# Another order of the engines' calls in the first block and the first two heads, and no filler transpositions outside the first loads

## The reference

```python
# layer 1: one causal attention head of width 256, with its own norm
x_norm = norm(x) * gamma + beta
q, k, v = x_norm @ qkv[:, :256], x_norm @ qkv[:, 256:512], x_norm @ qkv[:, 512:]
attn = softmax(causal(q @ k.T / 16))
x = norm(x + (attn @ v @ o_proj + x))
# layer 2: 16 causal heads of width 128 with rotary embedding, then 4 experts, top 2 of them
h = x + attention(norm(x) * ln1_w + ln1_b)      # q, k, v with biases; wo, bo
m = experts(norm(h) * ln2_w + ln2_b)            # gate, gelu(h @ we1 + be1) @ we2 + be2
x = norm(x + (h + m))
```

## Time and profile before

| | |
|---|---|
| runs | 1158.55, 1160.10, 1160.26 us |
| the profiled execution: first to last instruction | 1159.9 us |
| busy: PE, weight loads of PE (PEld), DVE | 1127.7, 1024.2, 860.5 us |
| busy: ACT, POOL | 735.7, 637.3 us |
| mean granted clock of PE | 0.991 |

### The profile page before, as it was taken

How to read it: one execution, slowest core, us unless ns; L and a number is a source line. 1 busy time by engine, 2 the same in 40 slices (tenths; PEclk the granted TensorE clock), 3 DMA queues, 4 the chain that set the end, 5 groups by cost and what they waited for, 6 DMA issues and landing times.

```text
span 1159.9 us, 20549 instructions
## 1 busy us (share of the span) xinstructions
PE 1127.7 (97%) x7183; PEld 1024.2 (88%) x7183; DVE 860.5 (74%) x2016; ACT 735.7 (63%) x1565; POOL 637.3 (55%) x511
## 2 busy tenths in 40 slices
PE   7998899999999999999999999999999999989996
PEld 6997889999999999899999999999999998778995
DVE  5865767777777777777777777777777777877698
ACT  3556676666666666666666666666666665665753
POOL 2306455565656565656555555665655555846673
PEclk8999999999999999999999999999999999989998
DMA  5002221221122111212121212121212111221001
GB/s 169 1 1 82 60 54 43 52 60 37 38 54 64 40 43 46 60 37 52 43 63 37 51 37 60 37 51 37 60 37 51 37 42 46 65 91 37 1 19 55
DMA packets 46301, 56.55 MB, mean 49 GB/s; under 512 B 5940, under 2 KB 29176, under 8 KB 46200
## 3 DMA queue, kind: packets, MB, share of 16 engines
q1 hardware_dynamic: 45368, 54.19, 18.9%
q10 hardware_dynamic: 832, 1.05, 0.3%
HBM read 17.47 MB, written 4.19 MB: 19 GB/s over the span
## 4 chain that ended last, share of the span: by engine, by line
PE 84%; DVE 7%; POOL 3%; issue 3%; ACT 1%; DMA 1%; SPq 0%; ACTq 0%; POOLq 0%; DVEq 0%
PE ps_m L424 52%; PE ps_s L424 20%; PE ps_t L566 11%; DVE acc L1664 2%; DVE acc L1674 1%; POOL work L2077 1%; DVE acc L1603 1%; POOL work L2081 1%; DVE stats L1442 1%; POOL qk_lo L2088 1%; PE ps_m L477 0%; DMA work<-in_L_attn_qkv 0%; DVE rows L1495 0%; POOL hT_lo L2059 0%; PE ps_m L628 0%
## 5 line engine op out<-in xcount | busy, mean ns | idle before, releaser
L2077 POOL TENSOR_TENSOR work<-work,rope 128x512 f32<-128x512 f32 x128 | 166.7, 1303 | 232.8 <-DMA work<-work 232.8
L1570 DVE TENSOR_TENSOR pT_lo<-ps_t,pT_hi 128x512 fp32r<-128x512 f32 (+3 forms) x408 | 210.4, 550 | 36.6 <-ACT pT_hi L1073 34.3
L1073 ACT ACTIVATE pT_hi<-ps_t 128x512 fp32r<-128x512 f32 (+3 forms) x408 | 183.0, 489 | 77.7 <-PE ps_t L566 77.5
L1563 DVE CUSTOM_DVE_ANT_0 ps_s<-ps_s,causal 128x128 f32<-128x128 f32 (+7 forms) x272 | 203.1, 766 | 5.7 <-PE ps_s L424 3.2
L2081 POOL TENSOR_TENSOR work<-work 128x512 f32<-128x512 f32 x128 | 167.4, 1308 | 10.1
L2088 POOL TENSOR_TENSOR qk_lo<-work,qk_hi 128x512 fp32r<-128x512 f32 x128 | 162.7, 1292 | 18.5 <-ACT qk_hi L1030 18.5
L1603 DVE SCALAR_TENSOR_TENSOR acc<-ps_m,rinv,acc 128x256 f32<-128x256 f32 x272 | 118.5, 477 | 71.8 <-PE ps_m L424 71.7
L1024 ACT ACTIVATE work<-ps_m,bqk 128x512 f32<-128x512 f32 x128 | 88.7, 693 | 108.7 <-PE ps_m L424 108.6
L1066 ACT ACTIVATE prob_b<-ps_s,nmax 128x640 f32<-128x640 f32 (+3 forms) x136 | 130.4, 959 | 22.3 <-DVE nmax L1563 19.0
L424 PE MATMUL ps_s<-qk_hi 128*128 128x384 f32 (+5 forms) x384 | 141.0, 367 | 2.0 <-POOL qk_lo L2088 1.1
L1524 DVE SCALAR_TENSOR_TENSOR work<-ps_m,bqk,rope 128x512 f32<-128x512 f32 x128 | 95.5, 746 | 56.3 <-ACT work L1024 56.1
(11 more groups left out here) (201 smaller groups left out, 2856.5 us busy)
## 6 DMA issues: line engine op xcount, KB each, us to landing
work<-work SPq DMA_DIRECT2D x256, 128.0 KB, 2.3
acc<-in_L_attn_x SPq DMA_DIRECT2D x8, 256.0 KB, 4.7
wst<-in_L_ffn_wq SPq DMA_DIRECT2D x16, 128.0 KB, 2.5
wst<-in_L_ffn_wk SPq DMA_DIRECT2D x16, 128.0 KB, 2.4
wo_st<-in_L_ffn_wo SPq DMA_DIRECT2D x16, 128.0 KB, 2.1
wst<-in_L_ffn_wv SPq DMA_DIRECT2D x8, 256.0 KB, 3.0
x_rows<-acc SPq DMA_DIRECT2D x4, 512.0 KB, 3.4
wst<-in_L_ffn_we SPq DMA_DIRECT2D x8, 256.0 KB, 2.8
```

The costliest lines, as they stand in the source:

```text
L1073: act.activation(pT_hi[:, slots, cols], t_bank(u, i, j)[:, 0:size * P].rearrange("p (j q) -> p j q", q=P), ACT.Copy).then_inc(t_hi.sem, t_ ...
L1563: dve.tensor_tensor_reduce(s, s, causal[:, T - (i + 1) * P:T], -1.0, ABOVE_ALL, ALU.add, ALU.min, accum_out=nmax[:, u % 2, i:i + 1]).then_ ...
L1570: dve.tensor_tensor(pT_lo[:, slots, cols], t_bank(u, i, j)[:, 0:size * P].rearrange("p (j q) -> p j q", q=P), pT_hi[:, slots, cols].bitcas ...
L2077: pool.tensor_tensor(qs[:, x % 2, :], qs[:, x % 2, :], sin_t[:, c * CH:(c + 1) * CH], ALU.mult).then_inc(sin_done.sem, sin_done.up(u, x))
```

## The change

All instructions but the filler ones stay, with the same operands. Their order in the `start()` list of each engine and of the SP queue is another. Of the fillers, the 14 and 28 of `fold_weight(0)` and `vectors(0)`, during the first loads, stay; 7 at `project_q(2, 2)`, 5 at `scores(33, 0)`, 13 at `outputs(33, 1)` and 4 at `gate_logits(0, 0)` go.

```diff
@@ PE, the fillers
                     if u == 2 and x % 2 == 0:
-                        if x == 2:
-                            keep_busy(out, 7)
                         await_hT(2, c)
...
-                if (u, i) == (LAST, 0):
-                    keep_busy(all_scores[:, score_bank(u, i)[0][0]:], 5)
...
-                if (u, c) == (LAST, 1):
-                    keep_busy(out, 13)
...
-                if (b, c) == (0, 0):
-                    keep_busy(out, 4)
@@ PE, start()
                 vectors(0)
                 fold_weight(2)
                 ln_transpose(0, 0)
-                vectors(1)
                 fold_product(3)
                 fold_product(4)
+                vectors(1)
                 project_q(0, 0)
                 project_q(0, 1)
                 ln_transpose(0, 1)
+                project_v(0, 0)
                 scores(0, 0)
+                project_v(0, 1)
                 scores(0, 1)
-                project_v(0, 0)
-                project_v(0, 1)
+                project_q(0, 2)
+                project_q(0, 3)
                 scores(0, 2)
...
                 ln_transpose(2, 0)
                 scores(1, 6)
+                first_outputs(1, 0, 1)
                 project_v(1, 3)
                 project_q(2, 0)
+                transposes(1, 4)
+                ln_transpose(2, 1)
                 scores(1, 7)
-                ln_transpose(2, 1)
+                project_q(2, 1)
                 transposes(1, 5)
-                project_q(2, 1)
                 project_q(2, 2)
                 project_v(2, 0)
                 transposes(1, 6)
                 first_outputs(1, 1, 0)
+                project_q(2, 3)
+                transposes(1, 7)
                 scores(2, 0)
+                project_v(2, 1)
                 scores(2, 1)
-                project_q(2, 3)
+                project_v(2, 2)
+                transposes(2, 0)
                 scores(2, 2)
...
@@ ACT, start()
                 high_proj()
-                high_qk_weights(0, 0)
                 ln_affine(0, 0)
...
+                ln_rows(2, 1)
                 exponent(1, 5)
+                high_v_weights(0)
                 high_values(1, 3)
                 add_bias(2, 0)
-                high_v_weights(0)
-                ln_rows(2, 1)
+                high_p(1, 4)
                 ln_affine(2, 1)
+                exponent(1, 6)
+                add_bias(2, 1)
                 high_p(1, 5)
-                add_bias(2, 1)
-                exponent(1, 6)
+                add_bias(2, 2)
+                high_qk(2, 0)
+                double(1, 1)
+                high_p(1, 6)
+                high_values(2, 0)
                 exponent(1, 7)
-                high_qk(2, 0)
-                add_bias(2, 2)
...
@@ DVE, start()
                 ln_stats(0, 0)
-                ln_stats(0, 1)
                 low_fold(0)
                 low_fold(1)
                 ln_apply(0, 0)
                 copy_vectors(0)
+                ln_stats(0, 1)
                 low_fold(2)
-                copy_vectors(1)
                 split_first(0)
                 low_fold(3)
                 low_fold(4)
+                copy_vectors(1)
                 ln_apply(0, 1)
...
@@ POOL, start()
                 ln_power(2, 0)
+                low_o_weights(0, 0)
                 ln_power(2, 1)
                 ln_low(2, 0)
+                ln_low(2, 1)
                 low_v_weights(0)
-                ln_low(2, 1)
+                turn(2, 0)
+                low_qk(2, 0)
+                turn(2, 1)
+                low_qk(2, 1)
                 ln_power(3, 0)
-                turn(2, 0)
-                turn(2, 1)
-                low_qk(2, 0)
-                low_qk(2, 1)
-                low_o_weights(0, 0)
...
@@ SP, start()
                 load_rope()
+                swap(2, 0)
+                keep_x1(0, 0)
                 load_v_weights(1)
                 load_qk_weights(0, 1)
-                swap(2, 0)
+                load_o_weights(0, 1)
                 swap(2, 1)
-                keep_x1(0, 1)
-                keep_x1(0, 0)
                 swap(2, 2)
...
```

More of the change, by code:

```diff
@@ L717, in start @@
                 scores(1, 4)
+                project_v(1, 2)
+                first_outputs(1, 0, 0)
                 transposes(1, 2)
@@ L736, in start @@
                 first_outputs(1, 1, 0)
+                project_q(2, 3)
+                transposes(1, 7)
                 scores(2, 0)
+                project_v(2, 1)
                 scores(2, 1)
-                project_q(2, 3)
+                project_v(2, 2)
+                transposes(2, 0)
                 scores(2, 2)
-                project_v(2, 1)
+                first_outputs(1, 1, 1)
                 scores(2, 3)
[L743 to L748, removed]
+                project_q(3, 0)
                 transposes(2, 1)
-                project_q(3, 0)
-                scores(2, 6)
                 project_v(2, 3)
                 transposes(2, 2)
+                scores(2, 4)
+                project_q(3, 1)
                 transposes(2, 3)
-                project_q(3, 1)
+                scores(2, 5)
+                scores(2, 6)
                 outputs(2, 0)
@@ L758, in start @@
                 ln_transpose(3, 0)
+                transposes(2, 5)
+                project_q(3, 2)
                 out_project(2, 0, 0)
-                project_q(3, 2)
+                scores(2, 7)
                 out_project(2, 0, 1)
[L762 to L765, removed]
                 project_q(3, 3)
                 project_v(3, 0)
+                scores(3, 0)
                 transposes(2, 6)
+                scores(3, 1)
                 ln_transpose(3, 1)
@@ L1182, in start @@
+                exponent(1, 1)
+                high_first(1, 3)
+                high_p(1, 0)
+                exponent(1, 2)
+                high_o_weights(0, 0)
+                exponent(1, 3)
+                high_values(1, 0)
+                high_p(1, 1)
+                high_values(1, 1)
+                high_values(1, 2)
+                ln_rows(2, 0)
                 exponent(1, 4)
-                double(1, 0)
                 high_p(1, 2)
                 high_p(1, 3)
-                high_values(1, 2)
@@ L1199, in start @@
-                exponent(1, 6)
-                exponent(1, 7)
-                high_qk(2, 0)
-                add_bias(2, 2)
-                high_values(2, 0)
+                add_bias(2, 2)
[3 more added lines that the diff above has]
+                high_values(2, 0)
+                exponent(1, 7)
+                high_qk(2, 1)
+                add_bias(2, 3)
+                high_p(1, 7)
+                exponent(2, 0)
+                high_values(2, 1)
@@ L1204, in start @@
+                high_values(2, 2)
                 high_qk_weights(0, 1)
-                high_qk(2, 1)
-                high_p(1, 6)
                 high_qk(2, 2)
-                add_bias(2, 3)
-                high_values(2, 1)
-                exponent(2, 0)
+                ln_rows(3, 0)
+                high_p(2, 0)
                 exponent(2, 1)
-                high_values(2, 2)
-                high_p(1, 7)
+                high_qk(2, 3)
                 exponent(2, 2)
+                add_bias(3, 0)
@@ L1788, in start @@
+                low_p(2, 4)
                 row_max(2, 6)
-                low_o(2, 0)
+                ln_apply(3, 1)
+                rotate(3, 2)
                 accumulate(2, 0, 0)
-                low_p(2, 4)
-                rotate(3, 2)
                 accumulate(2, 0, 1)
-                add_value_bias(0, 1)
                 row_max(2, 7)
-                row_max(3, 0)
                 low_p(2, 5)
                 rotate(3, 3)
-                invert(2, 1)
                 low_values(3, 0)
+                low_p(2, 6)
```

217 lines of the change are left out of this document (100 added, 117 removed).

## The result

The changed kernel takes 1149.55 us (median of six runs, 1149.16 to 1155.01), the kernel before 1159.42 us (six runs, 1158.33 to 1160.26). The ratio is 0.9927 with a 95% interval from 0.9914 to 0.9940. The gain is 9.9 us by the medians and 8.3 us by the means (1159.35 to 1151.03); the forecast was 6.3. Its 1153.6 us is 4 us too high, inside its range.

The account below looks back on a forecast made before the run. PE, busy 97% of the span, was taken as the bound, with 13.8 us idle in `start()` to win. 2.4 + 4.8 - 0.9 = 6.3 us off 1159.9 gave 1153.6 us, range 1148.3 to 1159.

Parts of the forecast that it names:

- I count from 1159.9 and correct nothing: Whole kernel: profiled span 1159.9 us, 0.2 below the median run of 1160.1, taken as the base without correction.
- The first 20 us: Start of `start()`: first projection at about 17.5 in place of 20.90, 3.4 us earlier; worth 2.4 after 1.0 for clock.
- The term for the clock: First stretch: a low-clock stretch as likely as not in the new order, so 1.0 of 2.0 us is given back.
- 20 to 165 us: Rest of `start()`: 8.2 us of PE idle time less 3.4 of new waits, a gain of 4.8 us.
- the single waits: PE between 20 and 165 us: new waits found call by call in the reordered lists, sum 3.4 us.
- the pair at `project_v(2, 0)`: `project_v(2, 0)` and `transposes(1, 6)` wait for `rotate(2, 1)` and `low_p(1, 5)` behind DVE's `ln_stats(3, 0)`: 0.6 us.
- no new waits: Rival for `start()`: the new waits are hidden and the first stretch has full clock; 11.6 us gained, 1148.3 us; chance 0.15.
- only the start wins: Rival: waits between 95 and 165 us move but do not shrink; 1.5 us gained, 1158.4 us; chance 0.18.
- the slow rival: Rival at `scores(2, 0)`: rotary chain of the first heads becomes the bound after a late `swap(2, 1)`; 1162.2 us; chance 0.07.
- no wait over 1.5 us: Sign for PE from 20 us to the end of `start()`: no wait longer than 1.5 us is left.
- the lead at the end of `start()`: Sign: prediction is wrong if the end of `start()` is not 4 to 10 us earlier.
- The fillers: Ends of the kernel: removing fillers starts nothing earlier, and one low-clock stretch at over even odds loses 0.9 us.

Follow-up runs that it names:

- e1: Kernel before with only the 29 fillers outside the first loads left out, old order kept; 1159.26 us, ratio 0.9999.
- the repeat: The changed kernel run and traced once more, unchanged; 1150.36 us, ratio 0.9930 to the kernel before.
- e3: Kernel before with the new order only up to the first two projections; 1157.86 us, ratio 0.9992.
- e2: Changed kernel with the 29 fillers put back in their four places; 1151.44 us, ratio 0.9933 to the kernel before.
- e4: Changed kernel with the old order put back up to the first two projections; 1153.03 us, ratio 0.9948 to the kernel before.

## Why the prediction was right, and where it was not

**The base: the step that says "I count from 1159.9 and correct nothing" failed.** I compared a span with a time. That execution took 1162 us, 2.6 us over the median, and 1.7 us of it are what its low-clock stretch before the first projection cost (e1). That this stretch lay in rows I had read (0.83 and 0.57) should have told me that this trace was no median one. Counted rightly, 6.3 us off 1162.0 would have been 1155.7 us; that the 1153.6 us on record lies nearer to the 1149.55 measured is luck.

**The first 20 us.** Forecast: 17.5 us for the first projection; measured 18.61, and 17.35 in the repeat. Counted from the first filler the forecast is 10.3 us, the two executions 10.9 and 10.3. The list was added up well enough, by two errors against each other: I left out that DVE's `copy_vectors(0)` waits 1.15 us for PE's fillers and that one small instruction of `ln_stats(0, 1)` takes 1.10 us in place of 0.17, and charged the whole 2.56 us of `ln_stats`, which had a wait of 0.47 us for a load in it. The 3.4 us that I gave to the order, however, are not the order's alone: 1.7 of them are the low clock of that one execution, and more is a bias load that landed late in it. At full clock the order brings some 0.5 us by the traces. The term for the clock failed too. I charged the new order half of 2.0 us for a low stretch of its own, "as likely as not"; none of the ten traces with a new first stretch has one before 21 us, and the timed runs have low-clock time less often with it, not more. The two errors work against each other: 3.4 - 1.0 = 2.4 us forecast, 1.2 to 1.7 us measured by the timed runs (e3 against e1, e2 against e4).

**20 to 165 us.** Forecast 4.8 us; measured 7.0 between e1 and e4. In the currency of the forecast, idle time, it is 4.9 for 4.8. The missing 2.1 us are time that the trace books as busy, most likely waits under the modelled ends. The match of the 4.8 is in part luck, since the single waits were mixed: `ln_transpose(2, 1)` 0.44 (forecast 0.7), the pair at `project_v(2, 0)` 1.37 (0.6). None came at `scores(0, 4)`, at `first_outputs(0, 0, ...)` or at `scores(2, 0)` (0.3, 0.3 and 1.0). An old wait of 0.43 us for `low_o`, at 140.66 before, stayed (131.98). The largest of all, 1.81 us, was not in my list: I gave `ln_apply(3, 1)` the 0.4 us per instruction of an idle POOL. The rivals "no new waits" and "only the start wins" fail by the earlier trace rows beside the rows of after; the slow rival too, as no `scores` of unit 2 waits for POOL: `swap(2, 1)` went out at 99.97, where I had 101.7, and `low_qk` was done at 108.5, where I had 109.2 and PE came at 109.56. Of the signs named beforehand, "no wait over 1.5 us" was not met, and the lead at the end of `start()` was inside 4 to 10 us in the first trace (9.6) and outside in the repeat (10.9).

**The fillers.** Forecast a loss of 0.9; measured 0.1 us of 1159 or nothing (e1, interval -1.2 to +0.9 us). The mechanism at their place was as told: PE, which was busy with 13 fillers for 1.63 us and then waited 0.63, waits 2.09 us at 1042.33. What was wrong is that this must lower the clock. In the first trace of the changed kernel the clock was low there, in the repeat, with the same wait (2.10 us at 1038.62), it was not, nor in e1 (2.06 us at 1046.29). The changed kernel over 1043.4 to 1046.6:
```profile
1043.40:1046.60 3.20, 3.20 (x9) 2.45 (x8) 2.17 (x5) 1.22 (x3) 2.80 (x3) 0.50 0.95 300
```
The repeat over 1030 to 1070:
```profile
1030.00:1070.00 40.00, 37.40 (x243) 33.38 (x242) 24.09 (x59) 25.02 (x42) 28.52 (x20) 1.00 0.09 28
```

**The sum, again.** 7.0 us for the order behind the first projections, 1.2 to 1.7 for the first stretch, 0 for the fillers: 8.2 to 8.7 us. The means of the changed kernel give 8.3 and 8.2 us in two sets of runs (1159.35 to 1151.03, 1159.15 to 1150.93), e2 against its own comparison 7.8 (1158.87 to 1151.08). The medians give 9.9 and 9.1 us because the executions fall into groups (those of e1: four at 1157.35 to 1157.55 us, seven at 1159.18 to 1161.47), so that a median jumps from one group to the other. The forecast of 6.3 us was short by 2.2 us from 20 to 165 us and by 0.9 us for the fillers, and about 1 us too high for the first stretch.

## What to carry to other kernels

Where one execution shows a low clock, price an order by its waits in an execution that lacks it, or by the time from a common event, before giving the time to the order. Look at the mean clock of every timed execution too: an order can make low stretches rarer, which one trace cannot show. Compare span with span and time with time. Before plain `tensor_scalar` instructions from SBUF to SBUF are put beside a busy POOL, charge each with up to one POOL instruction (here 4.46 us for four); a form that keeps off the shared port can be slower alone and still be the faster one there.

## What the runs showed of the hardware that was not expected

- A `tensor_scalar` of 128x256 between SBUF tiles takes 0.40 to 0.41 us with POOL idle and up to 1.39 us beside it. Four instructions of 128x4 in `ln_stats(3, 0)` and `ln_stats(0, 1)` go from 0.16 or 0.17 to between 0.99 and 1.23 us, six to seven times their length for four numbers per partition; one of them is a `tensor_tensor`, and each ends with the POOL instruction beside it. The RECIPROCAL between them stays at 0.18.
- The same program ran between 1149.2 and 1155.0 us. Its two traces are 1.3 us apart at the first projection (the fillers already start 0.7 us apart), still 1.3 at unit 3, and 5.3 at the end. The 4 us between are how long the clock was at its lower level from 990 to 1050 us, 0.89 against 0.97 (60 x 0.08 = 4.8); the repeat:
```profile
990.00:1050.00 60.00, 51.97 (x324) 44.71 (x323) 46.23 (x124) 39.34 (x81) 39.30 (x30) 0.97 0.26 80
```
- The same wait lowered the clock in one execution and not in another. Before its `first_outputs(1, 1, 0)` PE waits 2.37 us in the kernel before, 2.33 in e1 and 2.36 in e3. In the first two the granted clock stayed at 1.00; in e3 it fell towards the end of the wait (0.73 over 107.0 to 107.5 us) and stayed down to 110.7 us:
```profile
107.00:111.00 4.00, 3.44 (x17) 3.44 (x18) 1.11 (x2) 2.23 (x5) 4.00 (x4) 0.57 0.30 66
```
